# Blocks of 64 queries become blocks of 2 x 32, and the second norm's root moves to GpSimd

## The chip, the cores and the metric

The kernel runs on one core of a Trainium2 chip. The metric is the device time of one execution in microseconds. The core has TensorE (PE; its weight loads are listed apart, as PEld), VectorE (DVE), ScalarE (ACT), GpSimd (POOL) and SyncE (SP, which here only starts DMAs). TensorE reads SBUF and writes PSUM, of which there are eight banks of 512 floats a partition; the others carry the results out of PSUM.

## The reference

Four stages follow one another on an input of 4 x 256 x 128. The change is in the last one, six layers of attention over a window and a gated feed-forward. The stage works on 4 batches of 256 tokens that the code holds as `NB` rounds of `N` = 512 tokens (`TILES` = 4 tiles of 128), with 16 heads of 64. Cut to one layer:

```python
q, k, v = split(x @ Wqkv)                   # 16 heads of 64
q = l2norm(q) * qs ; k = l2norm(k) * ksc
q, k = rotary(q), rotary(k)                 # x*cos*scale + rotate_half(x)*sin*scale
# windows of 32: a query sees the keys of its own window and of the one before it,
# those from 32 positions back up to its own
sim = einsum('bhwie,bhwje->bhwij', bq, look(bk)) * 8 ; sim = where(mask, -big, sim)
out = einsum('bhwij,bhwje->bhwie', softmax(sim), look(bv))
x = x + out @ Wo
xs = shift_tokens(x)
xn = (xs - mean) / sqrt(var + 1e-5) * g + b
x = x + (a * gelu(gate)) @ W2 + b2          # a, gate = xn @ W1 + b1, 341 wide each
```

The second half of the features of `x` is shifted by one token ahead of both parts.

## The kernel before

Three stages come first (some 775 us); the window stage, `windowed_layers`, takes the rest. It does 24 **rounds**, 6 layers x 4 batches, and a round has these **units** (`T2.3` is kind, tile or block, part):

- `P`, `V` (L1766): the projection of one tile to 512 columns of q and k (`P`) or v (`V`), three matmuls (high and low parts of fp32), 24 units a round, into `psP`, which has two buffers.
- `Sq`, `AB`, `R`, `Ra`, `ad`, `nm`: ScalarE squares `psP`; VectorE multiplies it by the two rotary tables (L1914, L1915) and sums the squares (L1921); `Ra` is the chain of small operations for 1/sqrt of the q,k norms (`w_nrm`, L62 to L71); GpSimd adds the two products (`ad`, L2006) and multiplies by the norm (`nm`, L2011).
- `T`, `Te` (L1773; L1855, L1859): TensorE transposes 4 x 128 columns into `psT`, ScalarE copies them to `qT` or `kT`. 16 a round.
- `S` (L1783, L1789): scores of a block of 64 queries against 96 keys, for all heads. First the mask (`band_bf`) is multiplied into PSUM, then 16 matmuls of 64 x 64 x 96 follow. In PSUM 8 x 96 values stand on each of 128 partitions. 8 blocks a round.
- `Xm`, `Xe`, `Xd`, `Xn` (L1931, L1866, L1937, L2016): the row maximum (two of 4 x 96), the exponentials (8 of 96), the sums and their reciprocals, and GpSimd's division of `pb`.
- `At`, `Pt` (L1799, L1873): TensorE transposes the probabilities of half the heads into `psA`, ScalarE copies them to `pT`. 16 a round.
- `Av`, `Ot` (L1816, L1879): the values of half the heads, 8 matmuls of 64 queries; ScalarE copies `psO` out. 16 `Av` and 8 `Ot` a round.
- The tail, all of it through the one bank `psF`: `wo` (L1713), `xf`, `tr` (L1720, transposes of the shifted result), `ln` (statistics, a chain of ten small operations on `w_rs`, and the scaling, all VectorE), `back` (L1724), `xn`, `g`/`a` (L1734), `gg`, `h`, `w2` (L1738), `out`.

Each fp32 matmul is two in the trace; the projections and transposes are one each. Each engine works through a list of its own, `ORDER`, once for each round, and every dash behind a name sets the unit one round back. Semaphores carry the dependences. Nothing reorders the lists. SP starts the DMAs in its own list; `tl` loads all weights of the tail behind the last `out` of the layer before.

## Time and profile before

| | |
|---|---|
| median of 3 runs | 2547.62 us (2533.65 to 2552.36) |
| the profiled execution | 2536.73 us, its span 2535.0 us |
| PE busy | 2325.2 us, 92% |
| PEld, DVE, ACT, POOL busy | 66%, 79%, 73%, 50% |
| granted TensorE clock | 0.965 in the mean |

The profiled execution lies 0.4% under the median. Busy shares are of the whole span; in the first three stages POOL hardly works, so the stage must be read by itself. One matmul's record covers its way through the array, and records overlap: what a unit costs TensorE is the distance from its start to the start of the next.

### The profile page before, as it was taken

The numbers are of one execution on the slowest core, as the hardware profiler recorded it, in microseconds if no ns is written. First come the engines' busy times: TensorE is split into PE (matmuls) and PEld (weight loads), VectorE is DVE, ScalarE is ACT, GpSimd is POOL, SyncE is SP. The second block draws the span as 40 slices with busy tenths as digits, with TensorE's granted clock in tenths as the row PEclk, the third lists the DMA queues.
The fourth block names the chain that finished last, engine by engine and source line by source line (L and its number), as shares of the span: only waits on it lengthen the run. The fifth ranks groups of instructions, "written<-read, shape, count | busy, mean of one in ns | idle before, by whom it ended". The sixth has DMA issues, their size and how long they took to land.

```text
span 2535.0 us, 60549 instructions
## 1 busy us (share of the span) xinstructions
PE 2325.2 (92%) x22196; PEld 1663.6 (66%) x22196; DVE 2004.9 (79%) x4390; ACT 1850.2 (73%) x4176; POOL 1277.4 (50%) x1093
## 2 busy tenths in 40 slices
...
GB/s 86 9 2 1 44 69 75 75 75 67 27 22 77 35 30 38 25 39 56 41 39 33 52 41 27 39 25 56 41 39 39 50 35 33 27 51 44 25 29 21
DMA packets 37812, 103.90 MB, mean 41 GB/s; under 512 B 7953, under 2 KB 13393, under 8 KB 34705
## 3 DMA queue, kind: packets, MB, share of 16 engines
...
## 4 chain that ended last, share of the span: by engine, by line
PE 40%; DVE 16%; ACT 4%; issue 3%; DMA 3%; POOL 3%; SPq 1%; DVEq 0%; ACTq 0%; POOLq 0%
PE w_psP L1766 12%; PE w_psO L1816 6%; PE w_psF L1713 4%; PE w_psA L1799 4%; PE w_psF L1734 4%; PE w_psT L1773 3%; PE w_psS L1789 3%; DVE w_rs L67 2%; DVE w_bb L1915 2%; DVE w_ab L1914 2%; DVE w_sm L1937 2%; PE w_psF L1738 2%; PE w_psS L1783 1%; DVE w_mx L1931 1%; DVE w_nrm L1921 1%
## 5 line engine op out<-in xcount | busy, mean ns | idle before, releaser
L2006 POOL TENSOR_TENSOR w_ab<-w_ab,w_bb 128x512 f32<-128x512 f32 x384 | 491.9, 1284 | 210.5 <-DVE w_bb L1915 210.4
L2011 POOL TENSOR_TENSOR w_ab<-w_ab,w_nrm 128x512 f32<-128x512 f32 x384 | 397.7, 1052 | 125.1 <-DVE w_nrm L67 125.1
L1866 ACT ACTIVATE w_pb<-w_psS,w_mx 128x96 f32<-128x96 f32 x1536 | 391.2, 360 | 3.3 <-DVE w_mx L1931 2.6
L1842 ACT ACTIVATE w_sq<-w_psP 128x512 f32<-128x512 f32 x384 | 232.0, 604 | 157.5 <-PE w_psP L1766 152.1
L2016 POOL TENSOR_TENSOR w_pb<-w_pb,w_sm 128x768 f32<-128x768 f32 x192 | 282.4, 1471 | 111.6 <-DVE w_sm L1938 111.6
L1766 PE MATMUL w_psP<-w_hi,w_xh 128*128 128x512 f32 x576 | 300.6, 522 | 24.8 <-DVE w_bb L1915 12.2
L1914 DVE TENSOR_TENSOR w_ab<-w_psP,w_tabs 128x512 f32<-128x512 f32 x384 | 263.1, 685 | 63.9 <-ACT w_sq L1842 56.9
L1931 DVE TENSOR_REDUCE w_mx<-w_psS 128x4 f32<-128x384 f32 x384 | 201.7, 547 | 115.5 <-PE w_psS L1789 115.5
L1873 ACT ACTIVATE w_pT<-w_psA 128x512 f32<-128x512 f32 (+1 forms) x384 | 233.0, 607 | 64.0 <-PE w_psA L1799 63.2
L1921 DVE TENSOR_REDUCE w_nrm<-w_sq 128x8 f32<-128x512 f32 x384 | 258.7, 674 | 5.9 <-ACT w_sq L1842 3.8
L1915 DVE TENSOR_TENSOR w_bb<-w_psP,w_tabs 128x512 f32<-128x512 f32 x384 | 261.3, 681 | 0.0
L1180 DVE TENSOR_TENSOR e_glo<-e_hh,e_ghi 128x512 fp32r<-128x512 f32 x256 | 169.6, 687 | 92.9 <-ACT e_ghi L1134 92.8
L1773 PE MATMUL w_psT<-tables_all,w_ab 128*128 128x128 f32 x1536 | 234.4, 275 | 6.2 <-ACT w_qT L1855 4.4
L1799 PE MATMUL w_psA<-tables_all,w_pb 128*96 128x128 f32 (+1 forms) x1536 | 234.8, 276 | 5.4 <-ACT w_pT L1873 3.2
L1766 PE MATMUL w_psP<-w_hi,w_xl 128*128 128x512 f32 x576 | 230.3, 400 | 0.0
L1766 PE MATMUL w_psP<-w_lo,w_xh 128*128 128x512 f32 x576 | 230.2, 400 | 0.0
L1799 PEld LDWEIGHTS w_psA<-tables_all,w_pb 128*96 128x96 f32 (+1 forms) x1536 | 172.5, 134 | 78.2 <-issue 50.4
L1773 PEld LDWEIGHTS w_psT<-tables_all,w_ab 128*128 128x128 f32 x1536 | 182.7, 141 | 62.5 <-issue 18.3
L1128 ACT ACTIVATE e_hh<-e_psH,e_cols 128x512 f32<-128x512 f32 x256 | 175.8, 687 | 55.0 <-PE e_psH L1050 53.8
L1324 POOL MEMSET a_sc<- 128x256 f32 (+2 forms) x6 | 2.9, 525 | 384.9 <-POOLq L287 384.9
L1937 DVE TENSOR_REDUCE w_sm<-w_pb 128x8 f32<-128x768 f32 x192 | 181.5, 946 | 18.2 <-ACT w_pb L1866 15.1
L1713 PE MATMUL w_psF<-w_oT,w_o 128*128 128x512 f32 x384 | 174.8, 599 | 7.6 <-DMA w_cols<-in_cols_w 6.8
...
## 6 DMA issues: line engine op xcount, KB each, us to landing
...
```

Of the source, the lines that this page charges most:

```text
L1713: last = pe.matmul(psF[:, :], w_o[:, pair, :], oT[:, pair, :], start=(pair == 0), stop=(pair == PAIRS - 1), skip_group_check=True)
L1766: last = pe.matmul(psP[u % 2][:, :], x[r % 2][:, tt], w[:, layer % 2, ww], start=(n == 0), stop=(n == len(terms) - 1))
L1773: last = pe.transpose(psT[:, 128 * q:128 * (q + 1)], ab[:, k % 2, j, 128 * q:128 * (q + 1)], c.ident[:, :])
L1799: last = pe.transpose(psA[0:rows, 128 * q:128 * (q + 1)], pb[k % 2][:, 4 * j + q, :], c.ident[:, :])
L1866: last = act.activation(pb[k % 2][:, 4 * j + q, WIN * (k % 2):], psS[j][:, q * KEYS:(q + 1) * KEYS], ACT.Exp, bias=mx[:, 4 * j + q:4 * j + ...
L1873: act.activation(pT[0:rows, 4 * j:4 * j + 4, :], psA[0:rows, :].rearrange("p (a b) -> p a b", a=4), ACT.Copy).then_inc(s["pte"], 1)
L1914: dve.tensor_tensor(ab[:, k % 2, j, :].rearrange("p (h x d) -> p h x d", x=2, d=32), src, tab[0], ALU.mult)
L1915: dve.tensor_tensor(bb[:, i % 2, :].rearrange("p (h x d) -> p h x d", x=2, d=32), src[:, :, ::-1, :], tab[1], ALU.mult).then_inc(s["ab"], 1)
L1921: dve.tensor_reduce(nrm[k // 2][:, 0, 8 * (i % 8):8 * (i % 8) + 8], sq[:, i % 2, :].rearrange("p (h d) -> p h d", d=DH), AX_X, ALU.add).th ...
L2006: pool.tensor_tensor(a, a, bb[:, i % 2, :], ALU.add).then_inc(s["ad"], 1)
L2011: pool.tensor_tensor(a, a, nrm[k // 2][:, 1, 8 * (i % 8):8 * (i % 8) + 8].unsqueeze(2).to_broadcast([128, 8, DH]), ALU.mult).then_inc(s["n ...
L2016: pool.tensor_tensor(p, p, sm[k % 2][:, :].unsqueeze(2).to_broadcast([128, PAIRS, KEYS]), ALU.mult).then_inc(s["pn"], 1)
```

## The change

- A block is now 64 queries that come as two windows of 32, each against its own 64 keys: 8 x 64 values on a partition in place of 8 x 96. The scores are 32 matmuls of 64 x 32 x 64, the mask 8 of 32 x 32 x 256. The maximum is one operation, and the exponentials are 8 of 64.
- A block's probabilities are transposed in one `At` of 4 x 128 (before two), into `psT`, which they now share with the q,k transposes; `psA` is gone. `psO` takes two banks, `pT` has two buffers, and a block's `Av` is one unit of 32 matmuls with 32 columns moved (before two of 8 with 64).
- `v_even`, the values of the even blocks, has 128 rows and not 96.
- The root of the second norm (`w_rs`) goes from VectorE to GpSimd as twelve operations (`lr`); VectorE keeps the statistics (`ls`) and the scaling (`ln`). The rotary additions stay on GpSimd, the chain of the q,k norms on VectorE.
- `w_o` is loaded apart from the other weights of the tail, as soon as the last `wo` has read it.
- All five lists are new.

TensorE, from one `S` to the next, around the last part of the values; the lists before:

```order
L1783 MATMUL w_psS<-band_bf,ident_bf 64x384 x4
L1789 MATMUL w_psS<-w_kT,w_qT 64x96 x16
L1816 MATMUL w_psO<-w_pT,X 64x64 x8
L1766 MATMUL w_psP<-w_hi,w_xh 128x512
L1766 MATMUL w_psP<-w_hi,w_xl 128x512
L1766 MATMUL w_psP<-w_lo,w_xh 128x512
L1773 MATMUL w_psT<-tables_all,w_ab 128x128 x4
L1799 MATMUL w_psA<-tables_all,w_pb 128x128 x4
L1720 MATMUL w_psF<-tables_all,w_xsf 128x128 x4
L1773 MATMUL w_psT<-tables_all,w_ab 128x128 x4
L1799 MATMUL w_psA<-tables_all,w_pb 128x128 x4
L1816 MATMUL w_psO<-w_pT,X 64x64 x8
```

and now:

```order
L1813 MATMUL w_psS<-band_bf,ident_bf 32x256 x8
L1822 MATMUL w_psS<-w_kT,w_qT 32x64 x32
L1803 MATMUL w_psT<-tables_all,w_ab 128x128 x4
L1794 MATMUL w_psP<-w_hi,w_xh 128x512
L1794 MATMUL w_psP<-w_hi,w_xl 128x512
L1794 MATMUL w_psP<-w_lo,w_xh 128x512
L1851 MATMUL w_psO<-w_pT,X 64x32 x32
L1833 MATMUL w_psT<-tables_all,w_pb 128x128 x4
L1794 MATMUL w_psP<-w_hi,w_xh 128x512
L1794 MATMUL w_psP<-w_hi,w_xl 128x512
L1794 MATMUL w_psP<-w_lo,w_xh 128x512
```

Where two `At` and two `Av` stood for a block, one of each stands, with four times the matmuls in the `Av`.

VectorE at the second norm, before:

```order
L79 BN_STATS w_stats<-w_psF 128x6 x4
L81 BN_AGGR w_mv<-w_stats 128x2 x4
L62 SCALAR_TENSOR_TENSOR w_rs<-w_mv,w_halves 128x4
L63 SCALAR_TENSOR_TENSOR w_rs<-w_rs,w_guesses 128x4
L68 TENSOR_TENSOR w_rs<-w_rs 128x4
L67 SCALAR_TENSOR_TENSOR w_rs<-w_rs 128x4 x2
L71 TENSOR_TENSOR w_rs<-w_rs 128x4
L67 SCALAR_TENSOR_TENSOR w_rs<-w_rs 128x4 x3
L85 TENSOR_SCALAR w_yn<-w_psF,w_mv,w_rs 128x128 x4
```

and now, GpSimd from the addition ahead of the chain to the one behind it:

```order
L2054 TENSOR_TENSOR w_ab<-w_ab,w_bb 128x512
L81 TENSOR_SCALAR w_rs<-w_mv 128x4
L81 TENSOR_SCALAR w_rs<-w_rs 128x4
L84 TENSOR_TENSOR w_rs<-w_rs 128x4 x2
L81 TENSOR_SCALAR w_rs<-w_rs 128x4
L84 TENSOR_TENSOR w_rs<-w_rs 128x4 x3
L81 TENSOR_SCALAR w_rs<-w_rs 128x4
L84 TENSOR_TENSOR w_rs<-w_rs 128x4
L81 TENSOR_SCALAR w_rs<-w_rs 128x4
L84 TENSOR_TENSOR w_rs<-w_rs 128x4
L2054 TENSOR_TENSOR w_ab<-w_ab,w_bb 128x512
```

The ten operations on `w_rs` leave VectorE's list; GpSimd has twelve between `ad0.1` and `ad0.2`, and VectorE has three `AB`, two `Xd` and two `Xm` between `ls` and `ln`.

The diff, cut (the unchanged lines that stay as they were, the lists but for two pieces, and waits that only count anew are left out):

```diff
+def rsqrt_simple(eng, ch, y, x, half, tmp, first, op):
+    def two(out, in0, a, b, op0, op1):
+        ch.link(eng.tensor_scalar(out, in0, float(a), float(b), op0, op1))
+    def times(out, in0, in1):
+        ch.link(eng.tensor_tensor(out, in0, in1, ALU.mult))
+    two(half, x, first, 0.5, op, ALU.mult)
+    two(y.bitcast(I32), half.bitcast(I32), -0.5, GUESS, ALU.mult, ALU.add)
...
-    PAIRS, BLK = HEADS // 2, 64
-    KEYS = WIN + BLK
+    PAIRS, QB, KEYS = HEADS // 2, 32, 64
-    psA = c.ps("w_psA")
-    psS = [c.ps(f"w_psS{j}") for j in range(2)]
-    psO = c.ps("w_psO")
+    psS = c.ps("w_psS", (128, 2, 512))
+    psO = c.ps("w_psO", (128, 2, 512))
     ORDER = {
         "pe": """
...
+            P0.0 S3.0- T2.2- tr-- P0.1 T2.3- Av1.0- At2.0- P0.2 S4.0- T3.0- P0.3 Av2.0- At3.0- V0.0
+            S5.0- T3.1- V0.1 P1.0 Av3.0- T3.2- P1.1 back-- P1.2 T3.3- g0-- P1.3 S6.0- At4.0- V1.0 a0--
+            V1.1 S7.0- At5.0- Av4.0- At6.0- P2.0 g1-- Av5.0- T0.0 P2.1 a1-- At7.0- Av6.0- T0.1 g2-- T0.2
...
         "act": """
...
+            Xe3.0- Te2.3- Xe3.1- Sq0.1 Pt2.0- wh0.0 Sq0.2 Ot1.0- Te3.0- Xe4.0- Sq0.3 Xe4.1- Ot2.0-
+            Pt3.0- Ve0.0 Te3.1- Xe5.0- Sq1.0 Ve0.1 Xe5.1- Te3.2- Sq1.1 xn-- Sq1.2 Te3.3- gg0-- Sq1.3
+            Xe6.0-""",
...
                 elif kind == "T":
-                    wait(pe, s["te"], r * UR + 4 * k + j)
+                    if psT_free:
+                        pe.wait_ge(*psT_free[-1])
+                    psT_free.append((s["te"], r * UR + 4 * k + j + 1))
...
                 elif kind == "S":
+                    for c4 in range(4):
+                        for h in range(2):
+                            rows = slice(64 * h, 64 * h + QB)
+                            pe.matmul(psS[QB * c4:QB * c4 + QB, h, 0:4 * KEYS], c.ident_bf[rows, rows],
+                                      c.band_bf[rows, min(k, 1), :], start=True, stop=False, skip_group_check=True)
                     for g in range(2):
+                        for n in range(2):
+                            at = QB * (e + 2 * n)
+                            slot = KEYS * (2 * g + n)
+                            for c4 in range(4):
+                                for h in range(2):
+                                    rows = slice(64 * h, 64 * h + 64)
+                                    last = pe.matmul(psS[QB * c4:QB * c4 + QB, h, slot:slot + KEYS],
+                                                     qT[t % 2][rows, 4 * g + c4, at:at + QB],
+                                                     kT[rows, 4 * g + c4, 128 * t + at:128 * t + at + KEYS], start=False,
+                                                     stop=True, skip_group_check=True)
...
                 elif kind == "Av":
+                    for h in range(2):
+                        for c4 in range(4):
+                            for g in range(2):
+                                for n in range(2):
+                                    rows, head = slice(64 * n, 64 * n + 64), 2 * (4 * g + c4) + h
+                                    last = pe.matmul(psO[64 * g:64 * g + 64, n, QB * (4 * h + c4):QB * (4 * h + c4 + 1)],
+                                                     vals[rows, head * DH:(head + 1) * DH],
+                                                     pT[k % 2][rows, 2 * h + g, QB * c4:QB * c4 + QB], start=True, stop=True,
+                                                     skip_group_check=True)
...
+                elif k == "lr":
+                    ch = Chain(pool, s_root, 12, r)
+                    pool.wait_ge(s_stats, (r + 1) * 2 * TILES)
+                    rsqrt_simple(pool, ch, rs[:, 0, :], mv[:, :, 1], rs[:, 1, :], rs[:, 2, :], 1e-5, ALU.add)
+                    ch.end()
```

## Rows read from the trace of the kernel before

**Rows 1.** Windows: one round of the window stage, busy time by engine.
```profile
core 0: us, PE busy (x) PEld busy (x) DVE busy (x) ACT busy (x) POOL busy (x), PEclk, DMA share, GB/s
1502.11:1571.81 69.70, 68.09 (x787) 48.03 (x786) 61.68 (x127) 57.23 (x139) 51.06 (x42) 1.00 0.15 37
```

**Rows 2.** Waits of PE: engine line waited for, us in total, times, longest.
```profile
PE w_psF L1724 <- DVE w_yn L85: 28.3, 19, 4.6
...
PE w_psF L1720 <- DMA w_xsf<-H: 12.9, 9, 3.7
...
PE w_psF L1713 <- DMA w_cols<-in_cols_w: 6.8, 4, 2.2
```

**Rows 3.** Timeline of PE: start us, us, engine line op, out<-in xcount.
```profile
1500.44 0.60 PE L1773 MATMUL w_psT<-tables_all,w_ab 128*128 128x128 f32 x4
1500.88 0.60 PE L1799 MATMUL w_psA<-tables_all,w_pb 128*128 128x128 f32 x4
1501.23 0.48 PE L1766 MATMUL w_psP<-w_hi,w_xh 128*128 128x512 f32 x1
...
1502.11 0.36 PE L1783 MATMUL w_psS<-band_bf,ident_bf 64*64 64x384 bf16 x4
1502.29 0.83 PE L1789 MATMUL w_psS<-w_kT,w_qT 64*64 64x96 f32 x32
1503.05 0.50 PE L1766 MATMUL w_psP<-w_hi,w_xh 128*128 128x512 f32 x1
...
1504.29 0.60 PE L1799 MATMUL w_psA<-tables_all,w_pb 128*128 128x128 f32 x4
1504.82 0.69 PE L1816 MATMUL w_psO<-w_pT,w_v 128*64 128x64 f32 x16
1505.43 0.50 PE L1766 MATMUL w_psP<-w_hi,w_xh 128*128 128x512 f32 x1
```

**Rows 4.** Timeline of PE, the first matmuls of the program and transposes behind them.
```profile
7.77 3.55 PE L248 MATMUL m_ps<-m_sT,m_w 128*128 128x4 f32 x16
14.78 3.42 PE L298 MATMUL n_psX<-tables_all,X 128*128 128x128 f32 x16 [3.45 <-PEq L223]
```

**Rows 5.** Windows of PEld at the opening of an `S`: weight loads begun.
```profile
1502.05:1502.15 0.10, 0.05 (x8) 1.00 0.00 0
```

**Rows 6.** Timeline of ACT.
```profile
1511.63 0.59 ACT L1873 ACTIVATE w_pT<-w_psA 96x512 f32<-96x512 f32 x1
1512.11 1.03 ACT L1866 ACTIVATE w_pb<-w_psS,w_mx 128x96 f32<-128x96 f32 x4
1513.05 0.60 ACT L1842 ACTIVATE w_sq<-w_psP 128x512 f32<-128x512 f32 x1
```

**Rows 7.** Groups by line: count | busy us, mean ns | idle before.
```profile
L1931 DVE TENSOR_REDUCE w_mx<-w_psS 128x4 f32<-128x384 f32 x384 | 201.7, 547 | 115.5 <-PE w_psS L1789 115.5
L1921 DVE TENSOR_REDUCE w_nrm<-w_sq 128x8 f32<-128x512 f32 x384 | 258.7, 674 | 5.9 <-ACT w_sq L1842 3.8
L1937 DVE TENSOR_REDUCE w_sm<-w_pb 128x8 f32<-128x768 f32 x192 | 181.5, 946 | 18.2 <-ACT w_pb L1866 15.1
L1889 ACT ACT_TABLE_LOAD x47 | 60.3, 1283 | 0.8
L67 DVE SCALAR_TENSOR_TENSOR w_nrm<-w_nrm 128x64 f32<-128x64 f32 x240 | 54.1, 226 | 8.3
```

**Rows 8.** Timeline of DVE in the root of the second norm.
```profile
1540.38 2.21 DVE L67 SCALAR_TENSOR_TENSOR w_rs<-w_rs 128x4 f32<-128x4 f32 x2
1542.62 0.16 DVE L71 TENSOR_TENSOR w_rs<-w_rs 128x4 f32<-128x4 f32 x1
```

**Rows 9.** Groups by line of POOL.
```profile
L2011 POOL TENSOR_TENSOR w_ab<-w_ab,w_nrm 128x512 f32<-128x512 f32 x384 | 397.7, 1052 | 125.1 <-DVE w_nrm L67 125.1
L2016 POOL TENSOR_TENSOR w_pb<-w_pb,w_sm 128x768 f32<-128x768 f32 x192 | 282.4, 1471 | 111.6 <-DVE w_sm L1938 111.6
L954 POOL TENSOR_TENSOR la_ku<-la_kg 128x256 f32<-128x256 f32 x16 | 14.6, 916 | 82.4 <-ACT la_kg L829 82.4
L955 POOL TENSOR_TENSOR la_ku<-la_ku 128x128 f32<-128x128 f32 x16 | 10.1, 631 | 1.3
```

More of the change, by code:

```diff
@@ L74, in rsqrt @@
     fused(y, half, 5 * BETA ** 2, y, ALU.add)
+def rsqrt_simple(eng, ch, y, x, half, tmp, first, op):
[5 more added lines that the diff above has]
+    two(y.bitcast(I32), half.bitcast(I32), -0.5, GUESS, ALU.mult, ALU.add)
+    times(tmp, y, y)
+    times(tmp, tmp, half)
+    two(tmp, tmp, -2.0, STEP_A, ALU.mult, ALU.add)
+    times(y, tmp, y)
+    times(tmp, y, y)
+    times(tmp, tmp, half)
+    c1 = 2 * BETA * STEP_C ** 2
+    two(half, tmp, c1, -10 / 3 * BETA, ALU.mult, ALU.add)
+    times(half, half, tmp)
+    two(half, half, c1, 5 * BETA ** 2, ALU.mult, ALU.add)
+    times(y, half, y)
 def norm_tokens(c, dve, ch, out, src, stats, mv, rs, eps, consts=None):
@@ L1555, in windowed_layers @@
     s_ve = [c.sem(f"w_s_ve{j}") for j in range(2)]
-    s_norm, s_sum, s_f = (c.sem("w_s_chain_" + k) for k in ("norm", "sum", "tail"))
+    s_norm, s_stats, s_root, s_sum = (c.sem("w_s_chain_" + k) for k in ("norm", "stats", "root", "sum"))
     def load_scl(sp, layer):
@@ L1626, in windowed_layers @@
+        "dve": """
+            R2.3- R3.0- AB3.0- AB3.1- R3.1- out--- Xd0.0- R3.2- Xm1.0- R3.3- Ra1.0- AB3.2- Xd1.0- AB3.3-
+            Xm2.0- xf-- Xd2.0- Xm3.0- AB0.0 R0.0 ls-- Xd3.0- AB0.1 Xm4.0- R0.1 AB0.2 R0.2 AB0.3 Xd4.0-
+            Xm5.0- ln-- R0.3 AB1.0 Xd5.0- R1.0 AB1.1 R1.1 AB1.2 Xm6.0- AB1.3 R1.2 R1.3 Xd6.0- h0--
+            Xm7.0- Ra0.0 Xd7.0- h1-- AB2.0 R2.0 R2.1 AB2.1 AB2.2 h2-- AB2.3 Xm0.0 R2.2 tb0.0""",
         "pool": """
-            ad3.3-- nm2.1-- nm2.2-- nm2.3-- xl0.0 Xn1.0-- ad0.0- nm3.0-- ad0.1- Xn2.0-- nm3.1-- nm3.2--
@@ L1631, in windowed_layers @@
+            nm2.1- Xn1.0- nm2.2- nm2.3- nm3.0- ad3.2-""",
         "sp": """
[L1632 removed]
+            VE3.0-- VE0.0- xd0.0 VE1.0- t1-- tl- xfd-- wd0.0 VE2.0-""",
     }
@@ L1776, in step @@
                 elif kind == "S":
-                    t, half = k // 2, BLK * (k % 2)
+                    t, e = k // 2, k % 2
                     pe.wait_ge(s["te"], r * UR + 4 * t + 4)
-                    wait(pe, s["e"], r * UA + 2 * k)
-                    for g in range(2):
-                        for h in range(2):
-                            rows = slice(64 * h, 64 * h + 64)
-                            pe.matmul(psS[h][64 * g:64 * g + 64, 0:4 * KEYS], c.ident_bf[rows, rows],
-                                      c.band_bf[rows, min(k, 1), :], start=True, stop=False, skip_group_check=True)
```

161 lines of the change are left out of this document (77 added, 84 removed).

## The prediction

> **What bounds the kernel now.** I read the windows first. In an ordinary round of 69.7 us TensorE is busy 68.09, VectorE 61.68, ScalarE 57.23 and GpSimd 51.06 [rows 1]: TensorE sets the pace. Then its waits: over the whole run it waits 28.3 us for the second norm, 12.9 for the shifted rows and 6.8 for the tail's weights [rows 2], some 2 us of a round. So the time goes with what each unit costs TensorE, from its start to the next one's start [rows 3]. A transpose unit costs 0.44 (1500.44 to 1500.88), a projection 0.88, an `S` 0.94 (1502.11 to 1503.05), half an `Av` 0.61, and an `At` ahead of an `Av` 0.53.
>
> **What the change does, per round, on TensorE.**
> *Transposes.* 16 `At` become 8: 8 x 0.44 = 3.5 us less [rows 3].
> *Values.* Before, 16 instructions in two column halves of the array take 0.61. Four transposes move 512 columns in 0.44, 0.11 for 128, so 64 columns take 0.055; eight in turn are 0.44, and 0.17 is opening and closing. A block costs 2 x 0.61 = 1.22. Now 64 instructions go to four quarters of the array, 16 to each; each moves 32 columns (0.027) but loads 64. What a load costs by itself shows where almost nothing is moved: 16 matmuls of 4 columns, loads of 128, in 3.55 us, 0.21 apart, in a stretch where 16 transposes also take 3.42, 0.2 each and not 0.11 [rows 4]. At the later speed that is 0.11 for 128 columns and 0.053 for 64. So 16 x 0.053 + 0.17 = 1.02 if loads bind, 16 x 0.027 + 0.17 = 0.60 if moves do. I take 1.02, since the load is the longer: 8 x 0.20 = 1.6 us less. The bound is 5.0 less.
> *Scores.* Before, each quarter does 8 instructions of 96 columns, 8 x 0.083 = 0.66, and 0.10 goes on closing (1502.29 to 1503.05 is 0.76). Now each of eight tiles does 8 of 64 columns: 0.44 + 0.10 = 0.54. The mask falls from 384 columns (0.18) to 256 (0.12), but its tiles are of another shape than the scores', so I add a closing of 0.10. Together 0.76 for 0.94: 8 x 0.18 = 1.4 less.
> *Openings.* A unit on part of the array costs its forerunner 0.09 (0.53 against 0.44), and there are 8 fewer: 0.7 less.
> Sum 7.2 us a round; 24 rounds, 173 us.
>
> **Waits that go.** `back` now stands 18 units behind `tr`, about 13 us of TensorE's work (before 12 units and 7 us), and the chain of the second norm no longer runs on VectorE between GpSimd's operations. There two operations on `w_rs` took 2.21 us together while the next took 0.16 [rows 8]. I take 20 of the 28.3 us [rows 2]. `w_o` on its own removes the 6.8, since no `out` has to come first. Together 27.
>
> **Waits that come.** `psT` is now one bank for 24 units a round. A `T` or `At` must wait until ScalarE has copied the last one out. ScalarE starts a copy 0.48 after the operation before and four exponentials in 0.94 [rows 6], a little less with 64 columns; I take 0.8. Between `Te3.3` and `Pt4.0` stand `gg0`, `Sq`, two `Xe` and `Ve`, with two table loads of 1.28 [rows 7]: 0.6 + 0.5 + 1.6 + 0.5 + 2.6 = 5.8. From `T3.3` to `At5.0` that makes 0.2 + 0.5 + 5.8 + 0.5 + 0.2 = 7.2, while TensorE has 6.4 of its own (three units and `At4.0`, then four): 0.8 late. From `T3.0` to `T3.1` it is 0.3 in the same way. The other pairs come out even. 1.1 x 24 = 26.
> The lists are also tighter: GpSimd and VectorE each have work that can be late. GpSimd saves 8 x (1.47 - 1.05) = 3.4 in `Xn` and gains twelve small operations. No such one is in the trace; 128x128 takes 0.63 and 128x256 0.92 [rows 9], which falls to 0.35 for a narrow one, between 0 and 0.63: 4.2, or 0 to 7.6. It comes to 51.9, and its forced rest while it waits for the two q,k norm chains, 125.1 / 24 = 5.2 [rows 9], makes 57. Behind the chain stand `ad0.2`, `Xn4` and `nm3.3`, and for `ad0.2` waits `AB1.0`. `ad0.1` and the chain take 1.1 + 4.2 after VectorE's `AB0.1`, and VectorE has nine operations of some 0.6 ahead of `ln`, 5.4: even, and 3 late at the upper bound. VectorE falls by two maxima to one (8 x (1.09 - 0.67) = 3.4), by 8 x (0.95 - 0.67) = 2.2 in the sums [rows 7], and by about 5 of the chain, to 51. ScalarE loses 8 copies (3.8) and some 2 of exponentials, to 51. All three stay under TensorE's 61 to 63, by less on GpSimd than before. For this I add 1 us a round, 24; from nothing to 3 a round.
>
> **Sum.** 173 + 27 - 26 - 24 = 150 off the profiled 2536.7 is 2387. The median shown lies 0.4% above the profiled execution; I name **2390 us**. An ordinary round should be about 64 us.
>
> **Rivals.**
> *1, slower: TensorE is bound by instructions.* A block's 68 matmuls of mask, scores and values in the trace (4 + 32 + 32) become 136, and each has a load. The densest stretch has 32 in 0.66, 0.021 each [rows 3]. If that is a rate of instructions and not of columns, `S` costs 64 x 0.021 + 0.38 = 1.72 and `Av` 64 x 0.021 + 0.17 = 1.51: +6.2 + 2.3 - 3.5 - 0.7 = +4.3 a round, 103, and with the waits above (+23) 2663. It decides from 0.016 a matmul on, where the gain is used up. Against it: 8 loads begin within 0.05 us at the opening of an `S` [rows 5], and 0.083 for four instructions is what 96 columns ask for. Chance 0.14; with less of it, at 0.018, it would be about 2590.
> The Trainium skill (TensorE: Matmul & The Clock Gate, "Wait — 56ns, not 53.3ns?") says that matmuls never start less than about 25 ns apart, however few columns they move. By an estimate from that page `S` would be 2.0 and `Av` 1.8, and the time some 2770. The trace does not agree for matmuls on different parts of the array: 0.021 in the mean [rows 3].
> *2, no change: the q,k norm chain meets GpSimd.* An operation of VectorE with two SBUF operands took 1.1 where GpSimd worked and 0.16 later [rows 8], and the 18 operations a round on `w_nrm` take 0.23 [rows 7], as GpSimd rests there. If GpSimd, now fuller, is still at an addition or at `Xn` when `Ra` starts, each costs 0.75 more: 13.5 us a round on VectorE, 64, and with its waits the old 69. 2530. It takes GpSimd behind at both chains; the lists put `nm` behind each chain, so GpSimd soon runs dry. 0.08.
> The Trainium skill (SBUF — State Buffer, "SBUF: two separate sides") has this as an exclusive lock on a shared pair of ports, held for a whole instruction. By it a late GpSimd costs one operation and not nine, if its next one waits for the chain; by that alone this rival would be 2400.
> *3, a smaller gain: the lists give it back.* With `psT`, GpSimd and VectorE each late by 1 to 2 us a round more than I take, 3 to 4 in all: 2475. The work is 57 of 62 us on GpSimd, so this is easy. 0.19.
> *4, a larger gain: moves bind in `Av`.* 3.4 us less on TensorE, of which GpSimd's 57 and `psT` leave about 2: 2340. 0.13.
> The forecast has 0.43; the remaining 0.03 is a round longer for a cause I don't see.
>
> **Range and chances.** 2320 to 2600 leaves out the worst of rival 1 (about 0.1) and the best of 4 (about 0.05), and holds the load and move bounds and 0 to 7.6 for GpSimd's chain. 1% is about what a measurement of this kernel can tell from no change. Faster by more: 0.43 + 0.13 + 0.17 = 0.73. Within: 0.08 and the edge of 3, 0.10. Slower: 0.17.
>
> **What would show it.** Right: `S` starts to the next unit 0.76 later, `Av` 1.02; `w_rs` on POOL about 0.35 an operation; waits of `back` under 10 us; a few waits of `w_psT` for copies, near `At5.0`; rounds of 63 to 64 us. Wrong: score instructions even in distance at 0.02 and no groups of eight (rival 1); `w_nrm` operations near 1 us (rival 2); PE idle above 6 us a round (rival 3); `Av` at 0.6 (rival 4).

## The result, and the profile after

| | before | after |
|---|---|---|
| median | 2549.99 us (2533.65 to 2556.0, 4 runs) | 2447.79 us (2438.85 to 2452.55, 4 runs) |
| ratio, 95% interval | 1 | 0.9605 (0.9552 to 0.9658) |
| span of the profiled execution | 2535.0 us | 2436.2 us |

Faster by 4%, 102 us where 160 were named; 2448 lies inside 2320 to 2600.

The page of the kernel after: busy time and instructions, and the queue on which the engines' instructions arrive (packets, MB, share):

```profile
PE 2200.7 (90%) x34484; PEld 1561.3 (64%) x34484; DVE 1802.0 (74%) x3982; ACT 1722.6 (71%) x3982; POOL 1253.8 (51%) x1380
q8 instruction: 274, 4.49, 0.8%
```

Windows of one round, columns as in [rows 1]:

```profile
1505.95:1571.50 65.55, 61.87 (x1295) 43.37 (x1295) 50.98 (x107) 50.73 (x130) 48.06 (x54) 1.00 0.17 47
```

Against [rows 1] the round is 65.55 in place of 69.70; TensorE's busy time fell by 6.2 and the round by 4.2. Matmuls and loads went from 787 and 786 to 1295 each. TensorE's rest grew from 1.6 to 3.7. The others' busy time is 51, 51 and 48, where 51, 51 and 51.9 were forecast (the 57 for GpSimd counts 5.2 of forced rest).

Timeline of PE in this round, which answers to [rows 3]:

```profile
1505.95 0.30 PE L1813 MATMUL w_psS<-band_bf,ident_bf 32*32 32x256 bf16 x8
1506.18 0.86 PE L1822 MATMUL w_psS<-w_kT,w_qT 64*32 64x64 f32 x64
1506.97 0.66 PE L1833 MATMUL w_psT<-tables_all,w_pb 128*128 128x128 f32 x4
1507.38 0.47 PE L1794 MATMUL w_psP<-w_hi,w_xh 128*128 128x512 f32 x1
...
1511.03 0.30 PE L1813 MATMUL w_psS<-band_bf,ident_bf 32*32 32x256 bf16 x8 [1.01 <-ACT w_pb L1903]
...
1512.64 0.89 PE L1851 MATMUL w_psO<-w_pT,X 64*64 64x32 f32 x45
1514.54 0.54 PE L1851 MATMUL w_psO<-w_pT,X 64*64 64x32 f32 x19 [1.01 <-issue]
...
1517.14 1.14 PE L1851 MATMUL w_psO<-w_pT,w_v 64*64 64x32 f32 x64
1518.20 0.66 PE L1803 MATMUL w_psT<-tables_all,w_ab 128*128 128x128 f32 x4
```

An `S` costs 1.02 (1505.95 to 1506.97): the mask 0.23, the scores 0.79. Before it was 0.94 and 0.76 was forecast. An `Av` costs 1.06 where nothing disturbs it (1517.14 to 1518.20); 1.02 was forecast. But one `Av` stands still after 45 of its 64 matmuls, and what it waits for is "issue", nothing that the profile shows. And the `S` at 1511.03 waits for exponentials.

Waits of PE over the whole run (total, times, longest), which answer to [rows 2]:

```profile
PE w_psS L1813 <- ACT w_pb L1903: 27.1, 25, 2.5
PE w_psO L1851 <- issue: 22.9, 25, 2.2
PE w_psT L1803 <- POOL w_ab L2059: 21.1, 21, 4.5
...
PE w_psF L1749 <- DVE w_yn L1995: 6.2, 1, 6.2
...
PE w_psF L1745 <- DMA w_xsf<-H: 5.6, 5, 3.7
...
PE w_psS L1822 <- issue: 3.3, 6, 1.3
```

`back` (L1749) waits once, not 19 times, and the wait for the tail's weights is gone. In their place came 27 us for the exponentials of the block before, once a round; 21 for the norms' products; and 26 us of "issue" inside `Av` and `S`, which has no counterpart in [rows 2] or inside any such unit of the trace before.

The single wait of 1511.03 in ScalarE's own timeline:

```profile
1507.00 0.59 ACT L1878 ACTIVATE w_sq<-w_psP 128x512 f32<-128x512 f32 x1
1507.84 1.28 ACT L1903 ACT_TABLE_LOAD   x1 [0.25 <-DVE w_mx L1969]
1509.14 1.75 ACT L1903 ACTIVATE w_pb<-w_psS,w_mx 128x64 f32<-128x64 f32 x8
```

The `S` that waits is `S7`. There is one `psS`, so it needs all exponentials of block 6; these need the maximum, and behind it a table load of 1.28, since a Gelu (`gg0`) came before.

GpSimd's operations on `w_rs`, and VectorE's on `w_nrm` (the second rival), as groups:

```profile
L84 POOL TENSOR_TENSOR w_rs<-w_rs 128x4 f32<-128x4 f32 x168 | 33.8, 201 | 13.6
L67 DVE SCALAR_TENSOR_TENSOR w_nrm<-w_nrm 128x64 f32<-128x64 f32 x240 | 54.1, 225 | 8.3
```

0.20 for a narrow operation, not 0.35; and the q,k norm chain at 0.225, as in [rows 7].

### The profile page after: what moved, and what is told of

It reads as the page before. It is cut to its first block, busy times and chain, and to the rows that moved or that the text cites. A ratio compares the mean times of both kernels' runs of the same rounds, so it can differ in the third digit from the quotient of the medians.

```text
span 2436.2 us, 84263 instructions
## 1 busy us (share of the span) xinstructions
PE 2200.7 (90%) x34484; PEld 1561.3 (64%) x34484; DVE 1802.0 (74%) x3982; ACT 1722.6 (71%) x3982; POOL 1253.8 (51%) x1380
## 3 DMA queue, kind: packets, MB, share of 16 engines
q8 instruction: 274, 4.49, 0.8%
## 4 chain that ended last, share of the span: by engine, by line
PE 52%; DVE 7%; ACT 3%; issue 3%; POOL 2%; DMA 1%; SPq 0%; ACTq 0%; POOLq 0%; DVEq 0%
PE w_psP L1794 14%; PE w_psT L1803 8%; PE w_psO L1851 7%; PE w_psF L1738 6%; PE w_psS L1822 5%; PE w_psF L1760 4%; PE w_psT L1833 3%; PE w_psF L1764 2%; PE w_psS L1813 2%; ACT w_pb L1903 1%; ACT L1903 1%; DVE w_mx L1969 1%; POOL w_ab L2059 1%; DVE w_nrm L67 1%; DVE w_nrm L62 1%
## 5 line engine op out<-in xcount | busy, mean ns | idle before, releaser
L1903 ACT ACTIVATE w_pb<-w_psS,w_mx 128x64 f32<-128x64 f32 x1536 | 356.6, 332 | 27.6 <-DVE w_mx L1969 27.0
L1794 PE MATMUL w_psP<-w_hi,w_xh 128*128 128x512 f32 x576 | 274.8, 477 | 15.6 <-POOL w_xl L2044 8.5
L1803 PE MATMUL w_psT<-tables_all,w_ab 128*128 128x128 f32 x1536 | 246.0, 283 | 26.1 <-POOL w_ab L2059 21.1
L2069 POOL TENSOR_TENSOR w_pb<-w_pb,w_sm 128x512 f32<-128x512 f32 x192 | 200.7, 1045 | 122.7 <-DVE w_sm L1978 121.1
L1803 PEld LDWEIGHTS w_psT<-tables_all,w_ab 128*128 128x128 f32 x1536 | 174.4, 142 | 107.2 <-issue 42.6
L1891 ACT ACTIVATE w_qT<-w_psT 128x512 f32<-128x512 f32 x192 | 116.3, 606 | 154.2 <-PE w_psT L1803 153.9
L1976 DVE TENSOR_REDUCE w_sm<-w_pb 128x8 f32<-128x512 f32 x192 | 130.4, 679 | 83.5 <-ACT w_pb L1903 82.8
L1969 DVE TENSOR_REDUCE w_mx<-w_psS 128x8 f32<-128x512 f32 x192 | 130.9, 682 | 67.0 <-PE w_psS L1822 65.4
L1822 PE MATMUL w_psS<-w_kT,w_qT 64*32 64x64 f32 x12288 | 168.7, 226 | 3.5 <-issue 3.3
L1760 PE MATMUL w_psF<-w_hh,w 128*128 128x512 f32 (+1 forms) x288 | 156.3, 625 | 6.7 <-ACT w_yn L1927 3.8
```

What stands on the lines that cost most here:

```text
L1760: last = pe.matmul(psF[0:m, :], w_1[:, at:at + m], xn[:, :], start=True, stop=True)
L1794: last = pe.matmul(psP[u % 2][:, :], x[r % 2][:, tt], w[:, layer % 2, ww], start=(n == 0), stop=(n == len(terms) - 1))
L1803: last = pe.transpose(psT[:, 128 * q:128 * (q + 1)], ab[:, k % 2, j, 128 * q:128 * (q + 1)], c.ident[:, :])
L1822: last = pe.matmul(psS[QB * c4:QB * c4 + QB, h, slot:slot + KEYS], qT[t % 2][rows, 4 * g + c4, at:at + QB], kT[rows, 4 * g + c4, 128 * t + ...
L1903: last = act.activation(pb[k % 2][:, n, :], psS[:, j, KEYS * q:KEYS * (q + 1)], ACT.Exp, bias=mx[:, n:n + 1])
```

## The experiments

The time was to fall by 160 us and fell by 102. Two theories of the missing 58 us. **A**: TensorE itself costs more than priced, the scores by their instructions and then stalls of its instruction stream. **B**: the fixed lists give the gain back in waits between engines. Where nothing else is said, an experiment starts from the changed kernel.

### Where the stalls of "issue" stand: e1_shift

```diff
             pe.wait_ge(s["z"], 2)
+            for _ in range(64):
+                pe.matmul(psS[0:QB, 0, 0:QB], c.ident_bf[0:QB, 0:QB], c.band_bf[0:QB, 0, 0:QB], ...)
             turns(pe, "pe", step)
```

> TensorE begins the stage with 64 small extra matmuls, 128 instructions more with their weight loads; all the rest is the changed kernel. Theory A (the stream of TensorE's instructions arrives in packets of 16 KiB, and a group of 64 matmuls sometimes runs dry at the seam between two): the stalls inside the Av and S groups stay some 35 us in all, but stand at other instructions: counted in TensorE's own order, 128 places off from where they were, so in other units. Rival (they come from what the values' or keys' buffers are doing, a wait or a collision with a transfer): they stay in the same units of the same rounds, as the schedule is the same to 2 us. Time 2436 to 2450 in both.

Measured, in one run: 2443.49 us, waits of "issue" 21.6 in `Av` and 6.9 in `S`. How far the stalls are apart is told by windows from the end of one to the end of another. Kernel after:

```profile
1101.40:1115.08 13.68, 11.59 (x252) 8.21 (x252) 11.71 (x21) 12.33 (x30) 9.52 (x8) 1.00 0.01 3
1115.08:1158.80 43.72, 41.69 (x753) 28.26 (x754) 31.82 (x72) 30.79 (x76) 31.96 (x29) 1.00 0.25 69
...
1358.49:1514.52 156.03, 148.91 (x3147) 104.16 (x3147) 126.05 (x254) 125.20 (x314) 118.07 (x133) 0.99 0.17 48
```

and the shifted kernel:

```profile
1173.16:1186.95 13.79, 11.72 (x252) 8.29 (x252) 11.85 (x21) 12.09 (x29) 10.05 (x8) 1.00 0.01 4
1186.95:1230.10 43.15, 41.53 (x754) 28.13 (x753) 31.40 (x70) 30.65 (x76) 31.91 (x29) 1.00 0.21 60
```

Matmuls and loads between two stalls are 504, 1507 and 6294, which is 2, 6 and 25 times 252 to within 6. The page has 2 x 34484 of them and 274 packets on the instruction queue, 251.7 to a packet; 4.49 MB / 274 is 16.4 KB. So a stall stands where one packet of TensorE's instructions ends. In the shifted kernel the same series (504, then 1507) begins at 1173 and not at 1101, a round later, though nothing else was changed, which no wait of the schedule explains. Counted from the program's first matmul, though, the stalls of both fit one row of packet ends. Windows from the start of the program to the end of one stall, in the kernel after and in the shifted one:

```profile
0.00:1227.99 1227.99, 1071.78 (x11708) 788.41 (x11708) 892.14 (x2114) 819.48 (x1723) 403.88 (x440) 0.95 0.15 49
0.00:1230.11 1230.11, 1077.72 (x11709) 794.00 (x11709) 889.85 (x2113) 815.86 (x1719) 401.66 (x438) 0.95 0.15 49
```

These are 23416 and 23418 matmuls and loads, though 128 more go ahead in the second, and so it is another unit that stands still. What A expected of the units was only half right: they are others, but of the same kind and place in the round.

The packets themselves are in the trace. For the `Av` that goes on at 1514.54, this is all that moved from 1512.10 to 1513.10:

```profile
q8 instruction: 1, 0.02, 5.5%
```

This packet (16,384 bytes) starts at 1512.19 and lands at 1513.08. The kernel after has 28 stalls of over 0.25 us inside `Av` and `S`, and the shifted one has 28. At every one of them TensorE goes on 2.2 to 2.9 us after such a packet started and 1.2 to 1.6 us after it landed. Theory A holds as far as the stalls are concerned: TensorE waits for its instructions.

The Trainium skill (Runtime: NRT & Kernel Launch, "Instruction fetch mechanics") says that the stream comes in 16 KiB blocks and that crossing a block is mostly hidden. The trace agrees on the size. It does not agree on the cost: 26 us in all, up to 2.2 at a time in the kernel after. Before, with 32 recorded matmuls in a unit and not 64, the groups of L1789 and L1816 sat idle 0.4 us in all, with 180 packets on that queue.

### What the scores and values are bound by: e2_half_cols, e3_half_scores

The first moves 32 of each score matmul's 64 columns, and loads 32 of each value matmul's 64 (in both, four matmuls ahead of the stage fill `psO`, since parts of it are no longer written):

```diff
-    last = pe.matmul(psS[QB * c4:QB * c4 + QB, h, slot:slot + KEYS],
+    last = pe.matmul(psS[QB * c4:QB * c4 + QB, h, slot:slot + 32],
...
-                     kT[rows, 4 * g + c4, 128 * t + at:128 * t + at + KEYS], start=False,
+                     kT[rows, 4 * g + c4, 128 * t + at:128 * t + at + 32], start=False,
...
-    last = pe.matmul(psO[64 * g:64 * g + 64, n, QB * (4 * h + c4):QB * (4 * h + c4 + 1)],
-                     vals[rows, head * DH:(head + 1) * DH],
+    last = pe.matmul(psO[64 * g:64 * g + 32, n, QB * (4 * h + c4):QB * (4 * h + c4 + 1)],
+                     vals[rows, head * DH:head * DH + 32],
```

> Left out: each score matmul moves 32 of its 64 columns, and each value matmul loads 32 of its 64 columns; the number of instructions stays. Theory A, for the scores (now 0.79 us from the first to the next unit, forecast 0.54): TensorE's instructions bind, so they stay at 0.75 to 0.80. Rival (columns bind, and the closing was priced too low): 0.55 or less. For the values (now 1.07 with no stall): if loads bind, as the prediction had it, 0.65 to 0.85, down to where the instructions bind; if the instructions bind now, 1.07 as before. Time by A and loads: 24 x 8 x 0.3 = 58 us of TensorE less, 2385.

The second leaves out every second group of the scores, and moves 16 of the value matmuls' 32 columns:

```diff
-                    for g in range(2):
+                    for g in range(1):
                         for n in range(2):
                             at = QB * (e + 2 * n)
...
-    last = pe.matmul(psO[64 * g:64 * g + 64, n, QB * (4 * h + c4):QB * (4 * h + c4 + 1)],
+    last = pe.matmul(psO[64 * g:64 * g + 64, n, QB * (4 * h + c4):QB * (4 * h + c4) + 16],
                      vals[rows, head * DH:(head + 1) * DH],
-                     pT[k % 2][rows, 2 * h + g, QB * c4:QB * c4 + QB], start=True, stop=True,
+                     pT[k % 2][rows, 2 * h + g, QB * c4:QB * c4 + 16], start=True, stop=True,
```

> Left out: the scores of every second group of heads (16 of 32 matmuls), and each value matmul moves 16 of its 32 columns. Scores: theory A (0.012 an instruction, 64 of them) 0.79 falls by half of that, to 0.40; rival (columns and a closing of 0.3 or more) to 0.5 or 0.55. Values: loads bind, 1.07 as before; moves or their number of columns bind, 0.8. Stalls at the seams of the instruction stream fall a little with 24 x 8 x 64 fewer instructions (some 12% of TensorE's).

Timeline of PE, half the columns:

```profile
1523.43 0.76 PE L1851 MATMUL w_psO<-w_pT,w_v 64*32 64x32 f32 x64
1524.12 0.30 PE L1813 MATMUL w_psS<-band_bf,ident_bf 32*32 32x256 bf16 x8
1524.35 0.76 PE L1822 MATMUL w_psS<-w_kT,w_qT 64*32 64x32 f32 x64
1525.04 0.50 PE L1794 MATMUL w_psP<-w_hi,w_xh 128*128 128x512 f32 x1
```

and half the score instructions, with half the columns of `Av` moved:

```profile
1515.92 0.46 PE L1822 MATMUL w_psS<-w_kT,w_qT 64*32 64x64 f32 x32
1516.31 0.66 PE L1803 MATMUL w_psT<-tables_all,w_ab 128*128 128x128 f32 x4
...
1536.09 1.12 PE L1851 MATMUL w_psO<-w_pT,tables_layer 64*64 64x16 f32 x64
1537.14 0.66 PE L1833 MATMUL w_psT<-tables_all,w_pb 128*128 128x128 f32 x4
```

Half the columns take the scores from 0.79 to 0.69, half the instructions to 0.39. `Av` falls from 1.06 to 0.69 with half the columns loaded, and with half the columns moved it lost about 0.01. At full size it is bound by loads, as forecast: its matmuls start four at a time, every 0.059 us, and 0.053 was named.

For the scores, 0.39 as half of 0.79 looks like a fixed price of 0.012 for a matmul with its load. But e3 halves their columns and loads with them, and the starts inside a unit show that the pace isn't even. Windows of the matmuls and loads of L1822 alone, for the first part of an `S`, in the kernel after and with half the columns:

```profile
1506.17:1506.42 0.25, 0.24 (x32) 0.24 (x33) 1.00 0.00 0
1524.34:1524.53 0.19, 0.18 (x32) 0.18 (x33) 1.00 0.00 0
```

The first 32 matmuls start within 0.24 us, in groups of eight every 0.056, as the prediction had it for 64 columns; with 32 columns they start within 0.18. Then 0.08 us pass, the last 31 take 0.32, about 0.010 each, and the next unit starts 0.15 after the last of them. In e2 the last 28 of an `S` and the last 32 of an `Av` go at 0.010 and 0.009 each, nearly the same pace, though only half of the columns are moved or loaded. In e3 the unit ends with its 32nd matmul: 0.24 + 0.15. So columns set the first half of an `S`, and in the second half something that hardly depends on them, the instructions by their number or the way they are passed on; 0.012 is only the mean. It would fit that some 32 lie ready when a unit starts and the rest are taken as they come; no run tests this.

The times are the surprise: 2423.32 and 2395.45 us, one run each. e2 took 8 x (0.10 + 0.37) = 3.8 us a round off TensorE's units, 90 us, and the kernel gained 24, where 2385 was expected. Its waits rose: for the norms' products from 21.1 to 42.0, "issue" from 26.2 to 40. e3 took 8 x 0.40 a round, 77 us, and gained 52. There the stream of instructions is thinner, and "issue" inside `Av` and `S` is gone from the waits. So work taken off TensorE alone counts for a fraction.

A part of what is missing is the granted clock. In windows of 3 us, from 800 us to 40 us before the end, it stood at its lower level (0.50, 1.2 GHz) for 26 us in the kernel after, but for 55 in e2 and 58 in e3. In e2 the five of 22 rounds (from one `tr` to the next) with such a stretch (5.5 us of it in the mean) took 67.7 us and the others 64.8, so a microsecond of it costs about half of itself. If both runs follow one line (saved = a x work + b x "issue"), a is 0.40 and b 0.82; with the clock counted in at that price, 0.57 and 0.92. That is an estimate from two single runs for two unknowns, which nothing checks.

### One unit moved: e4_s7_later

```diff
-            V1.1 S7.0- At5.0- Av4.0- At6.0- P2.0 g1-- Av5.0- T0.0 P2.1 a1-- At7.0- Av6.0- T0.1 g2-- T0.2
+            V1.1 At5.0- Av4.0- S7.0- At6.0- P2.0 g1-- Av5.0- T0.0 P2.1 a1-- At7.0- Av6.0- T0.1 g2-- T0.2
```

> Only TensorE's list: S7.0 stands behind At5.0 and Av4.0 and not ahead of them. In the changed kernel S7.0 waits 1.1 us in nearly every round (27.1 us in 25 times) for the exponentials of block 6, which ScalarE starts late. Theory B (the lists give part of the gain back): the wait goes, and 20 to 27 us with it: 2410 to 2428. Theory A (these waits were covered, instructions bind): the maximum and the exponentials of block 7 are later by as much and At7.0 or the second round's units wait instead: 2440 to 2450.

2500.9 us, ratio to the kernel before 0.9836 (0.9813 to 0.9858): 53 us slower than the change, which neither theory had. The wait at `S7` went, but waits of PE now read

```profile
PE w_psT L1833 <- ACT w_pT L1909: 45.6, 24, 2.9
```

`At5` wants the single `psT`, which is free only when ScalarE has copied out `Pt4`; and that stands behind both `Xe6`. `S7` had been waiting for the same stretch of ScalarE. This is the wait that the prediction placed at `At5.0` for 0.8 a round; in the changed kernel `S7`'s wait had hidden it. It is also longer than `S7`'s, and the clock adds to it. Windows of 900 to 2400 us in the kernel after and in e4, and one stretch of e4:

```profile
900.00:2400.00 1500.00, 1422.48 (x29146) 983.76 (x29144) 1163.79 (x2385) 1156.86 (x2894) 1095.62 (x1190) 0.99 0.18 49
900.00:2400.00 1500.00, 1418.61 (x28390) 982.12 (x28390) 1130.85 (x2357) 1132.81 (x2840) 1083.60 (x1177) 0.97 0.17 49
...
1545.00:1551.00 6.00, 4.75 (x104) 3.76 (x97) 2.12 (x8) 1.56 (x8) 0.89 (x1) 0.50 0.39 113
```

Just ahead of this stretch TensorE had stood still 1.89 us for `At5`. An `At` inside it costs 0.77 (1548.57 to 1549.34), and 0.42 a few units earlier. In e4, 14 of 22 rounds have such a stretch and take 69.0, the other eight 67.9; rounds without one take 66.1 in the kernel after. So the clock makes some 10 to 15 of the 53 us, and the wait the rest.

### The table loads: e5_gelu_together, e8_no_gelu

e5, each of the tail's six steps of `g`, `a` one place later, and with them `gg` and `h`:

```diff
-            V1.1 S7.0- At5.0- Av4.0- At6.0- P2.0 g1-- Av5.0- T0.0 P2.1 a1-- ...
+            V1.1 S7.0- g0-- At5.0- Av4.0- At6.0- P2.0 a0-- Av5.0- T0.0 P2.1 g1-- ...
```

> The changed kernel with the gate's three steps (g, gg, a, h) each one place later in the lists, so that ScalarE does all three Gelus in one stretch: two table loads a round and not four, and none between the squares and the exponentials of block 6. S7.0 waits there 1.1 us in every round, and where TensorE's own work was cut by 3.8 us a round (half of the score and value columns left out) the round fell by less than 1. Theory B (the lists bind: a chain S6 to maximum to table load to exponentials to S7 sets the round): the wait at S7.0 goes and the round falls by 1 to 2 us, 2400 to 2425. Theory A (TensorE's instructions and stalls bind): the freed microsecond comes back as waits of at most the same places and the time stays, 2435 to 2450. Third: psF is now late, w2 or wo waits for h2 and it is slower, over 2450.

e8, from the change again:

```diff
-                    act.activation(gg[0:m, :], psF[0:m, :], ACT.Gelu, bias=cols[0:m, 5 + n:6 + n])
+                    act.activation(gg[0:m, :], psF[0:m, :], ACT.Square, bias=cols[0:m, 5 + n:6 + n])
```

> Left out: the window stage's gate takes a square in place of the Gelu, so ScalarE never has to load a table there (93 loads of 1.28 us in the changed kernel). All lists stay. Theory B (ScalarE's chain at S7 and the tight lists bind): S7's wait goes (27 us) and more, 2390 to 2415. Theory A (TensorE binds by its instructions and stalls): at most 2435.

e5: 2606.51 us, ratio 1.0242 (1.0209 to 1.0274), slower than the kernel before. The loads did halve (23 for the Gelus and 22 for the exponentials, before 46 and 45) and `S7` hardly waits, but two waits of PE took over (and 21 of 22 rounds now have a stretch at the lower clock, 162 us in all against 26, so that at half of itself the clock makes some 50 to 70 of the 159 us lost):

```profile
PE w_psF L1760 <- ACT w_yn L1927: 100.4, 49, 3.5
PE w_psP L1794 <- DVE w_bb L1953: 38.8, 52, 1.0
```

`a0` stood where `g1` had been, ahead of its own Gelu in ScalarE's list. e8: 2423.01 us, 0.9509 (0.9493 to 0.9526), 25 us faster. Freed of 117 us of loads (59.0 + 57.7 in the groups of the kernel after), the kernel gains about what `S7` waited (27.1, now 2.9) and no more.

### Two parts by themselves: e6_split_load, e7_root_on_vector

e6, from the kernel before:

```diff
+    def load_out(sp, layer):
+        wait(sp, s["f"], (layer * NB - 1) * 10 + 1)
+        sp.dma_start(w_o[:, :, :], c.ins["w_o1"][layer]).then_inc(s["wo"], 16)
...
-            VE1.0--- xfd---- VE2.0--- xd0.0 VE3.0--- VE0.0-- wd0.0- tl---""",
+            VE1.0--- xfd---- to--- VE2.0--- xd0.0 VE3.0--- VE0.0-- wd0.0- tl---""",
```

> The kernel before with one part of the change: w_o loaded apart from the rest of the tail's weights, as soon as its last reader is done. The prediction gave this part 6.8 us (its wait in the trace). If right: ratio 0.996 to 0.998, some 7 us; the rounds at a layer's start, 72 to 74 us, come nearer to the others' 70. Rival: the wait goes over to the next weights (w_1) or to other units, ratio 0.999 to 1.001.

2531.83 us, 0.9934 (0.9914 to 0.9954). The wait for the weights went. The gain is 17 us by the ratio, 12 to 22 by its interval, and so more than the 6.8 forecast; the two profiled spans (2535.0 and 2529.9) differ by only 5. What the rest of the gain is stays open.

e7, the root in VectorE's `ls`, and `lr` off GpSimd's list:

```diff
+                    rsqrt(dve, ch, rs[:, 0, :], mv[:, :, 1], rs[:, 1, :], rs[:, 2, :], 1e-5, ALU.add, (halves, guesses))
...
-            ... Xn3.0-- ad0.1- lr--- ad0.2- ...
+            ... Xn3.0-- ad0.1- ad0.2- ...
```

> The changed kernel with the second norm's root back on VectorE, behind its statistics, the lists otherwise the same. By the prediction the move to GpSimd was worth most of 20 us of waits of back. If so: nine operations of 0.16 to 1.0 stand ahead of Xd3 and AB0.1, and the time rises by 10 to 40 us, 2458 to 2490. Rival: the time went with back's later place in the list, and VectorE has room (51 of 66 us): within 5 us, or faster by up to 10, since GpSimd loses 4 us a round.

2473.41 us, 0.9709 (0.969 to 0.9727): moving the root is worth some 26 us (20 by the ratios, against e12, the change measured again below). Not by `back`, though, which waits once here too. Here waits of PE have

```profile
PE w_psP L1794 <- DVE w_bb L1953: 25.8, 25, 2.0
```

in place of 5.9: with nine more operations (nine, in the kernel before too, not the ten told above) VectorE is late in freeing `psP`. The clock has a part in it, with 53 us at its lower level against 26. And the nine are cheap here:

```profile
L67 DVE SCALAR_TENSOR_TENSOR w_rs<-w_rs 128x4 f32<-128x4 f32 x120 | 19.5, 162 | 4.1
```

In the kernel before, the same operations took 450 ns in the mean. In the round that I looked at, GpSimd rests from 1509.87 to 1512.69 and the nine run from 1509.92 to 1511.65.

### The order alone: e9_lists, e10_lists_half, e11_lists_2, e12_again

Nothing but `ORDER` differs. To find an order, I let each engine work through its list on paper, with the durations read from these traces and the kernel's own waits, and moved a unit where that made the round shorter. TensorE's list of e11:

```diff
-            P0.0 S3.0- T2.2- tr-- P0.1 T2.3- Av1.0- At2.0- P0.2 S4.0- T3.0- P0.3 Av2.0- At3.0- V0.0
-            S5.0- T3.1- V0.1 P1.0 Av3.0- T3.2- P1.1 back-- P1.2 T3.3- g0-- P1.3 S6.0- At4.0- V1.0 a0--
-            V1.1 S7.0- At5.0- Av4.0- At6.0- P2.0 g1-- Av5.0- T0.0 P2.1 a1-- At7.0- Av6.0- T0.1 g2-- T0.2
-            P2.2 a2-- T0.3 P2.3 Av7.0- S0.0 V2.0 T1.0 V2.1 P3.0 T1.1 P3.1 w2-- S1.0 T1.2 P3.2 P3.3 T1.3
-            wo0- At0.0 wo1- T2.0 V3.0 S2.0 T2.1 V3.1 Av0.0 At1.0""",
+            P0.0 S3.0- T2.2- P0.1 tr-- T2.3- P0.2 Av1.0- At2.0- S4.0- T3.0- Av2.0- P0.3 At3.0- V0.0 S5.0-
+            T3.1- V0.1 P1.0 T3.2- Av3.0- T3.3- back-- P1.1 P1.2 g0-- S6.0- P1.3 At4.0- a0-- V1.0 V1.1 S7.0-
+            At5.0- Av4.0- At6.0- g1-- P2.0 Av5.0- P2.1 T0.0 a1-- At7.0- Av6.0- T0.1 g2-- P2.2 T0.2 P2.3
+            Av7.0- T0.3 a2-- V2.0 T1.0 V2.1 S0.0 P3.0 P3.1 T1.1 w2-- P3.2 S1.0 P3.3 T1.2 wo0- T1.3 wo1-
+            At0.0 S2.0 T2.0 V3.0 V3.1 T2.1 Av0.0 At1.0""",
```

The other lists change in the same way (on ScalarE `Pt4` goes ahead of `Ve1.0`, and `Sq1.3` and `Xe6.0` follow `gg0` as before). e9 is an earlier stage of the same search; e10 is e9 with e2's edit.

> The changed kernel with the four compute lists in another order and nothing else: units stand one to three places earlier or later, so that a wait of one engine meets less often the work that another still has ahead of it. Theory B (with these shapes the lists bind and not TensorE's work; a cut of 3.8 us of TensorE's work a round gave 1.2): the waits of TensorE for the exponentials (27 us) and for the norms' products (21 us) fall to under 15 us together, rounds of 63 to 64.5 us and 2370 to 2410. Theory A (instructions of the scores and stalls of the instruction stream bind): the time stays within 15 us of 2448.

> The same lists, and left out as before: each score matmul moves 32 of its 64 columns, each value matmul loads 32 of its 64. On the lists of the change this took 3.8 us a round off TensorE's units and 1.2 us off the round. If theory B holds and the new lists leave TensorE as what binds, it now takes 2.5 to 3.8 us off the round, 60 to 90 us against the run with the same lists. If something else still binds, again 1 to 1.5 us.

> The changed kernel with a second set of lists, worked over further than the first: g1 stands behind At6, Xe7.1 behind Pt6, V2 ahead of S0, so that TensorE's waits for the exponentials nearly go. If waits in the lists still hold the round: 2415 to 2430. If the round is now TensorE's own work plus the stalls of its instruction stream (some 62 and 1.5 us), no order can give more than the first set did: 2430 to 2440.

> The changed kernel once more, unaltered, on the same chip as the lists above: to see what the two sets of lists are worth against it. Its ratio was 0.9605 with an interval of half a per cent to each side; expected 0.957 to 0.963. The first set of lists gave 0.9595, so the two may be equal: then the waits that the lists took away came back elsewhere.

| | us | ratio to the kernel before |
|---|---|---|
| e9 | 2436.86 | 0.9595 (0.9575 to 0.9614) |
| e10 | 2409.55 | one run |
| e11 | 2413.63 | 0.9492 (0.9462 to 0.9521) |
| e12, the change again | 2447.47 | 0.9630 (0.9600 to 0.9660) |

e9 gained 11 us against e12 (9 by the ratios), which is what A expected and not B. Taken alone it would have closed the question wrongly: e11, on the same chip as e12, gained 34: the same work, 1.4% faster than the change by its order. It is the fastest kernel here that leaves nothing out, 5.1% under the kernel before. Its waits of PE:

```profile
PE w_psP L1793 <- DVE w_bb L1952: 24.6, 58, 1.7
PE w_psO L1850 <- issue: 8.7, 13, 1.4
...
PE w_psS L1812 <- ACT w_pb L1902: 5.9, 23, 1.9
```

The exponentials' wait fell from 27.1 to 5.9, that for the norms' products is no longer among the large ones, "issue" from 26.2 to 11; VectorE's products (24.6 for 5.9) are later, and a wait of `At` for the copies of keys (6.7) is new. So the second branch of what was expected, that no order could beat e9, was wrong, and 2413.63 lies just below the 2415 to 2430 of the first. e10 answers the other question: on e9's lists, 90 us less work of TensorE again gave only 27. The clock has no part here (27 and 31 us at its lower level), "issue" inside `Av` and `S` rose from 14 to 24, and VectorE's products from 19.1 to 25.3. No engine is the bound by itself even there.

## Why the prediction was right, and where its size was off

*The direction* was right for the reasons given: fewer transposes and openings, shorter values, `back` and `w_o` freed. The size was not: 102 us for 160, within a range wide enough to hold it.

*Scores (failed).* "A block's scores in 0.54 + 0.22", 1.4 us a round less. They take 0.79 + 0.23, so 0.6 more than before: 2.1 a round on TensorE, 50 us. The step that failed is "each of eight tiles does 8 of 64 columns: 0.44". It holds for the first 32 matmuls (0.24 for half of it); the other 32 take 0.40 for 0.22, 35 of the 50 us, and the closing is 0.15 for 0.10. I read [rows 5] (8 loads within 0.05 us) as a rate that holds. Rival 1 was nearer in kind, a limit that isn't the columns, but not in its rate: 0.021 was its price, and 0.016 where it was to decide. Its own sign was that the groups of eight would be missing; they are there in the first half of a unit and not in the second.

*Values (right).* 1.06 for 1.02, bound by loads; e2 and e3 show it from both sides. That rules out rival 4: 0.60 was not to be had, since 64 matmuls with half the columns loaded still take 0.69.

*The instruction stream (not in the forecast).* 26 us of stalls inside `Av` and `S`, where a packet of instructions ends. Before, 2 x 22196 matmuls and loads came in 2535 us, now 2 x 34484 in 2436.

*Waits that go.* 20 of 28.3 for `back`: it was 22; 6.8 for the weights: gone. But that GpSimd's root is what freed `back` was not so: in e7 the root is back on VectorE, and `back` still waits once. What is left is its later place in the list.

*Waits that come.* 50 us in two terms (26 for `psT`, 24 for tighter lists); 48 came, in two waits. That the sums agree is luck, since the places were wrong: `S7` waits for `psS`, and `T0` for GpSimd. The prediction's own place, `At5.0` behind `Pt4.0`, is real but lay under `S7`'s wait, and e4 uncovered it. GpSimd's chain takes 0.20 an operation, inside 0 to 0.63.

*Rival 2* fell: `w_nrm` stays at 0.225. *Rival 3* is nearest in its mechanism: 2475 was its price, 2448 the time, and e11 shows 34 us of it in the order alone. Its sign, over 6 us of rest a round, was not met: 3.7.

*The sum.* With the measured terms it would be 173 - 50 - 8 (8 x 0.04 x 24) = 115 of work, less what waits added. All waits of TensorE for and inside the stage's units make 92.9 us before and 119.8 after, 27 more: the terms above add more than that, but the shifted rows (12.9 to 5.6) and VectorE's products (12.2 to 5.9) were waited for less, and so was ScalarE (19.2, now 6.7 beside the wait of `S7`). That leaves 88, where the two profiled executions differ by 92 in the window stage (it starts at 776.3 and at 769.8, so that 6.5 of the 99 between the spans come from the stages that weren't changed). The lower clock, 10 us before and 26 after, takes some 8 more, so about 12 us stay unexplained. The forecast promised too much, then, by the scores (50 us) and by the waits: 23 us more of them were to come than to go, and with the lower clock it was some 35. How strongly waits grow as work is taken off TensorE is seen in e2 and e10, where it went into the time at 0.3, not at 1. How much of the 58 us goes to the scores and how much to the stalls is therefore only estimated: with 0.40 and 0.82 from above 20 and 21, with 0.57 and 0.92 28 and 24.

*Left open:* why the packet comes late at some ends and not at others. Most ends lie inside `Av` or `S`, since these are over 80% of TensorE's instructions, and most pass without a stall. The stretch 1148 to 1159, at the end of which an `Av` stands still, has transfers of 110 GB/s; 1170 to 1181, with 364 matmuls and loads and so at least one packet's end, has next to none and no stall:

```profile
1158.82 0.65 PE L1851 MATMUL w_psO<-w_pT,tables_layer 64*64 64x32 f32 x27 [1.89 <-issue]
```

```profile
1148.00:1159.00 11.00, 9.11 (x289) 7.08 (x289) 7.21 (x20) 8.37 (x26) 10.07 (x11) 1.00 0.41 110
1170.00:1181.00 11.00, 9.95 (x183) 6.65 (x181) 9.96 (x19) 10.58 (x25) 7.49 (x7) 1.00 0.01 3
```

That data transfers hold up the instructions would fit these two, but it isn't the whole of it. From 1505.3 to 1515 only two packets of instructions moved and no data at all, and the stall of 1.01 us that ends at 1514.54 lies there. At 6 of the 28 no data moved from 2.5 us ahead of the packet on. On the other hand the share of the DMA engines that was busy around the 28 packets is 0.32 in the mean, and 0.18 around all packets of the stage. The packets at stalls took no longer than others once they moved (median 1.12 and 1.07 us), so if something holds them up, it is ahead of their start. No run moved a transfer to try it. Nor did one test why TensorE slows down behind the 32nd matmul of an `S`.
